# Waits between pairs of row sends on GpSimd, from token group 4 on

## What is computed

```python
x = x + _L0_gnn_ref(_layernorm(x), adj, ...)   # 4-head graph attention, normalised by degrees
x = x + _L0_ffn_ref(_layernorm(x), ...)        # top-2 of 8 experts for each token
x = x + _L1_gnn_ref(_layernorm(x), adj, ...)   # one-head graph attention
x = x + _L1_ffn_ref(_layernorm(x), ...)        # mixture of experts by batch, then a layer norm
```

```python
gate_scores = x @ Wg + bg
_, idx = jax.lax.top_k(gate_scores, K)          # K = 2
mask = jax.nn.one_hot(idx, E, dtype=x.dtype).sum(axis=-2)
h = jax.nn.gelu(jnp.einsum('td,edh->teh', xf, W1) + b1[None], approximate=False)
y = jnp.einsum('teh,ehd->ted', h, W2) + b2[None]
out = jnp.einsum('ted,te->td', y, mf)
```

## Time and profile before

| | us |
|---|---|
| median of 3 runs | 698.01 (694.73 to 698.65) |
| the profiled execution: its time | 696.12 |
| its span in the trace | 694.4 |
| PE busy in the span | 620.4 (89%) |
| DVE, ACT, POOL busy | 524.3, 470.7, 357.3 |
| sends (L1240), 64 of them | 63.8 busy on POOL |
| scatters (L1914), 91 of them | 87.3 busy on POOL |

### The profile page before, as it was taken

How to read it: one execution, slowest core, us unless ns; L and a number is a source line. 1 busy time by engine, 2 the same in 40 slices (tenths; PEclk the granted TensorE clock), 3 DMA queues, 4 the chain that set the end, 5 groups by cost and what they waited for, 6 DMA issues and landing times. The chain is left out here.

```text
span 694.4 us, 18433 instructions
## 1 busy us (share of the span) xinstructions
PE 620.4 (89%) x5349; PEld 523.8 (75%) x5349; DVE 524.3 (76%) x2268; ACT 470.7 (68%) x1286; POOL 357.3 (51%) x585
## 2 busy tenths in 40 slices
PE   7798998998998968799999999995799889999993
PEld 5455666665665636799999999994788879989993
DVE  6899899999999997675444444445999931998898
ACT  6578898889889743566666666662267767657661
POOL 1135455777777785755445554455532107746440
PEclk9899999999999996599999999999999979999998
DMA  6349323444321111522764544316993001032122
GB/s 172 98 129 178 107 79 107 133 136 153 107 87 63 63 35 50 139 66 69 186 151 145 148 130 132 96 52 125 228 245 139 15 1 63 3 90 62 31 62 62
DMA packets 75796, 71.80 MB, mean 103 GB/s; under 512 B 7782, under 2 KB 64770, under 8 KB 74930
## 3 DMA queue, kind: packets, MB, share of 16 engines
q1 hardware_dynamic: 62194, 51.12, 26.6%
q0 software_dynamic: 11200, 13.35, 7.9%
q10 hardware_dynamic: 2304, 6.16, 3.2%
HBM read 44.06 MB, written 26.54 MB: 102 GB/s over the span
## 5 line engine op out<-in xcount | busy, mean ns | idle before, releaser
L1914 POOL DMA_INDIRECT expert_outputs<-y_rows,y_at x91 | 87.3, 959 | 83.5 <-DVE y_rows L1886 77.1
L1678 ACT ACTIVATE hT<-psum,b1blk 128x128 f32<-128x128 f32 x280 | 79.8, 368 | 41.4 <-PE psum L1590 41.4
L1590 PE MATMUL psum<-xinT,w1blk 128*128 128x128 f32 x728 | 98.9, 280 | 1.2 <-DVE w1blk L1867 1.2
L1612 PE MATMUL psum<-f_w,hT 128*128 x728 | 96.1, 276 | 0.0
L1590 PEld LDWEIGHTS psum<-xinT,w1blk 128*128 128x128 f32 x728 | 91.1, 197 | 1.6 <-issue 1.6
L1612 PEld LDWEIGHTS psum<-f_w,hT 128*128 128x128 f32 x728 | 88.7, 192 | 0.1
L1867 DVE TENSOR_SCALAR w1blk<-f_w 128x256 f32 x182 | 47.4, 302 | 44.7 <-issue 41.9
L892 DVE TENSOR_TENSOR adj_h<-psum,adjT 128x1024 f32<-128x1024 f32 x64 | 76.6, 1215 | 1.5 <-ACT psum L678 0.2
L1240 POOL DMA_INDIRECT pair_rows<-rows,row_of x64 | 63.8, 997 | 27.0 <-issue 14.5
L678 ACT ACTIVATE psum<-psum 128x1024 f32<-128x1024 f32 x64 | 64.1, 1007 | 15.2 <-PE psum L427 15.2
L2547 PEld LDWEIGHTS psum<-w2s,hT 128*128 128x128 f32 x512 | 62.0, 192 | 3.2 <-ACT hT L2619 1.6
(11 more groups left out here) (366 smaller groups left out, 1503.4 us busy)
## 6 DMA issues: line engine op xcount, KB each, us to landing
adj_in<-in_adj_dram SPq DMA_DIRECT2D x32, 256.0 KB, 3.9
adjT_scratch<-adjT SPq DMA_DIRECT2D x32, 256.0 KB, 2.8
adjT<-adjT_scratch SPq DMA_DIRECT2D x6, 1024.0 KB, 5.1
xin<-pair_rows SPq DMA_DIRECT2D x91, 64.5 KB
xres<-in_x_dram SPq DMA_DIRECT2D x16, 256.0 KB, 3.8
b2wide<-b_of_blocks ACTq DMA_DIRECT2D x7, 512.0 KB
xres<-expert_outputs POOLq DMA_DIRECT2D x6, 512.0 KB, 8.8
out_dram<-yout SPq DMA_DIRECT2D x6, 512.0 KB, 3.8
```

The source lines that it names most:

```text
L1590: ins = nc.tensor.matmul(psum[:, HIDDEN_BANKS + n % 2, lo:lo + P], w1blk[:, u, k, c * P:(c + 1) * P], xinT[:, u, :], start=True, stop=True)
L1612: ins = nc.tensor.matmul(psum[:, OUT_BANKS + n % 2, 0:D], hT[:, u, k, c, :], flat[:, bass.ds(places[k] + (HID + c * D), D)], start=(k == 0 ...
L1678: ins = nc.scalar.activation(hT[:, u, k, c, :], psum[:, HIDDEN_BANKS + n % 2, lo:lo + P], ACT.Gelu, bias=first_bias[:, c, k, i:i + 1])
L1914: pool.indirect_dma_start(y_dram[:, :], bass.IndirectOffsetOnAxis(ap=y_at[:, u:u + 1], axis=0), y_rows[:, u, :], None).then_inc(s_y_sent[u ...
```

## The change

After each part of a group from 4 on, POOL waits until that part's two sends have landed. The semaphore's value in the wait counts all earlier groups on it and this group's sends so far, so it is this part's sends that the wait is for.

```diff
@@ -1240,6 +1240,8 @@
                     pool.indirect_dma_start(
                         rows_dram[:, :], bass.IndirectOffsetOnAxis(ap=row_of[:, g % NROWS, t:t + 1], axis=0),
                         rows[:, g % NROWS, t, :], None).then_inc(s_sent[g % NROWS], 16)
+                if g >= IN_DRAIN - 1:
+                    pool.wait_ge(s_sent[g % NROWS], SENT[g - NROWS] + 16 * TB * (part + 1))
 
             def sends(s):
 
```

## The result

The kernel with the waits takes 711.13 us in the median of 4 runs (708.82 to 714.19), the kernel before 697.91 on the same chip (4 runs, 694.73 to 698.65): a ratio of 1.0202 [1.0176, 1.0229]. That is 13 to 14 us slower where 9.0 were forecast. The sign and the chain of waits were right; the size was not, because a term was missing from the sum. On the scale of the 698.01 us shown ahead of the prediction the result is 698.01 x 1.0202 = 712.1, just beyond the range.

What follows compares the result with a forecast made beforehand. The prediction took the DVE-POOL chain to bound stage 1's drain and PE to bound stage 2. Late start 3.7, first scatter 3.1 and scatters behind group 8 2.2 made 9.0 us: 698.0 + 9.0 = 707.0 us, range 701.0 to 712.0.

Steps and rivals of the forecast that it cites:

- Sum: Whole kernel: late start of stage 2 plus two stops inside it, 3.7 + 3.1 + 2.2 = 9.0 us, giving 707.0 us.
- Longer stops: Rival, stage 2: later landings beside the spreads give 710.6 us, or a lower PE clock in a stop 712; chance 0.13.
- Price of one wait: POOL's sends: waiting for a landing costs 2.4 + 0.3 - 1.27 = 1.4 us of POOL per wait.
- Term 1: Start of stage 2: five waits delay batch 29's add_attention and so DVE's statistics, starting the stage 3.7 us later.
- The late loads: SP's first load moves 9.2 us later, to 282.5 us, covered by PE's idle time before 286.77 us.
- Term 2: First scatter, issued at 309.7 us instead of 294.48: DVE waits 3.3 us for its landing, PE loses 3.1 us before block 10.
- Term 3: Scatters behind group 8: block 5's goes out at 323.9 us, DVE waits 2.65 us, PE loses 2.2 us.
- The rival without stops: Stage 2: sends beside the spreads land in 2.4 us, so no stop of PE or one; 703.4 us, chance 0.22.
- the packets of the earlier trace: Sign for late landings beside the spreads: POOL's queue moved 32 packets, one send, in 281 to 284 us with three issued.
- Faster: Rival: short waits move add_attention(28) away from DVE's small instructions, gaining 2.2 us; 695.8 us, chance 0.05.
- hidden: Rival: DVE reaches batch 29's statistics later or landings are quicker, and scatters are in time; 698 to 701.5 us, chance 0.10.

Runs made afterwards that it cites:

- the five stops: Kernel before with PE made to wait for a scatter's landing ahead of five blocks, another chip: idle 747.41 us (1.0308), filled with useless matmuls 742.20 us (1.025).
- w45: Changed kernel with the waits of groups 4 and 5 alone: 702.75 us against 696.46 for the kernel before, 1.0079.
- w8: Changed kernel with the waits of group 8 alone: 698.06 us against 697.55 for the kernel before, 0.9998.
- warm_b: Kernel before with useless matmuls in PE's two gaps at the start of stage 2, repeated with 12 runs: 695.89 us against 696.89, 0.9989.

## Why the prediction was wrong

The step that failed is the **Sum**: 3.7 + 3.1 + 2.2 counts only the time for which PE stands still, as if it went on at full speed afterwards. That put the fall of the clock at nothing. It stood in a rival, *Longer stops*, added to stops longer than those of the forecast and with a chance of 0.13. It belonged to the forecast's own stops. Behind stops of 4.1 and 2.3 us the trace has stretches at the lower clock that cost 1.5 and 3.2 us, and the five stops show that such a stretch costs time of its own. With them the forecast would have been 9.0 + 4.7 = 13.7 us, near the 13.2 of the medians. Step by step:

- **Price of one wait**, 1.4 us: right. The gaps are 1.4 to 1.8 us instead of 0.30, but for three behind late landings (2.46, 4.68 and 3.56). The estimate of 2.15 us for a transfer, worked out from the Trainium skill, page "DMA: Bandwidth & Descriptors", section "Anatomy of one DMA — SWDGE (gpsimd) path", would have made them shorter; the 10 sends of 258 to 283 us land 2.3 to 3.2 us after their start, median 2.4.

```profile
DMA to landing us min/median/max: 2.3/2.4/3.2
```

- **Term 1**, +3.7: 4.0 at L1727 and 4.3 at the hidden layer of block 0. Right in its chain. It was a little low because L1210 of batch 29 ends at 269.06 + 1.05 = 270.1 on the old scale instead of 269.8. Of it 0.9 came back with the clock.
- **The late loads**: right. SP's first load is issued at 281.44, on the old scale 282.5 as forecast, and PE waits 0.16 us for it:

```profile
283.98 0.48 PE L1580 MATMUL psum<-ident,xin 128*128 128x128 f32 x1 [0.16 <-DMA xin<-pair_rows]
```

- **Term 2**, +3.1: 4.1. Here luck helped. The forecast has the second and third pair of group 6 late, at 5.8 us each from start to start, and the others at 3.9 to 4.0. It was the first and second that were late, at 286.99 - 282.32 = 4.67 and 6.91; the third took 3.81. The six pairs of groups 6 and 7 took 27.15 us together, where the forecast has 27.35. Group 6 began 1.0 us later than forecast, so the first scatter is at 310.5 on the old scale (309.7 forecast). DVE was there 0.2 us sooner, and so it waited 4.20 us instead of 3.3. The size is right to within 1 us; the 1.5 us at the lower clock are what was left out.
- **Term 3**, +2.2: 2.3 for the stop. The scatter of block 5 came 2.7 us later than forecast, as a pair of group 8 took 5.79 us instead of 3.9, but by then DVE was later too. The 3.2 us of slow stretch behind it were left out.
- **The rival without stops** (703.4): out, since both stops are there; the packets of the earlier trace rows were the better sign, though only one pair came as late as they suggest. **Faster** and **hidden**: out, by w45 and by DVE's 2.86 us before L881.

What stays open: why the lower clock lasts twice as long behind the second, shorter stop (6.8 us against 3.4), and whether the later stretches of the profiled execution, in stages 2 and 3, come from the change or belong to its being the slowest run. Other kernels speak for the second: w8, which is as fast as the kernel before, also waits 2.43 us for a late load and has 3.4 us at the lower clock behind it, and warm_b, also as fast, begins stage 3 with 10.2 us at the lower clock. Waits that ask for the pair before the last, or one wait a group, would tell the latency of a landing from the number of sends in flight; no run here gives a time for either.

## What to carry to other kernels

A wait for a transfer's landing costs its latency less what would have been issued meanwhile, 1.4 us here, but what that does to the end depends on who stands behind: group 8's waits alone cost nothing, and 0.6% behind the others. Follow the chain to the next engine's order and to the ring that limits it. A ring lets the waits through unseen until its depth is used up, and then each further microsecond is a stop of the busiest engine. To a stop of a saturated TensorE add the price of the clock behind it (here 1.4 to 1.6 us for each 3.4 us at the lower level), as a term of the sum and not as a rival.

## What was not expected of the hardware

- Useless matmuls in stops that are there anyway make a program faster: 5.2 us in the medians over five stops, four of them about 3 us long.
- Nearly equal stops had different results. In the kernel with five idle ones the stop of 2.89 us was followed by the lower clock and that of 2.87 us was not; in the changed kernel the stop of 2.34 us was. So no length of a stop between 2.3 and 2.9 us can be called safe or unsafe from these runs.
- Indirect sends behind the wide spreads landed up to 5.7 us after their start (the 12 sends of 282 to 310 us: least 2.3, median 2.5), and single ones elsewhere came late by about 2 us without a spread beside them (group 8's pair above, with loads of `xin` alone). A chain that waits for each pair takes every one of these delays in full; in the kernel before, POOL waits for no landing there.
